# A two-layer image kernel: the last window group in a PSUM bank of its own, and a new order of TensorE's steps

## The chip, the cores and the metric

One Trainium2 chip, one of its cores. The metric is device microseconds for one execution of the whole program, the median of several runs.

## What is computed

Input is 16 images of 128 channels and 56x56 pixels. Layer 0, which the change is in, does this to each image:

```
x   = x + depthwise3x3(x)
y   = layernorm over channels(x)
q, k, v = y @ qkv_w + qkv_b
idx = for each of 49 windows (8x8 pixels) the 4 windows with the largest q_mean . k_mean
att = softmax(q_window . k_of_those_4_windows, per head, 4 heads)       # 64 x 256 per window and head
o   = att @ v_of_those_4_windows
o   = (o + depthwise5x5(v)) @ wo_w + wo_b                                # "lepe"
x   = x + o
x   = x + gelu(layernorm(x) @ mlp_w1 + mlp_b1) @ mlp_w2 + mlp_b2
```

Layer 1 begins with a 3x3 convolution, which is done in the same loop over images. The rest of it (a state-space scan over the pixels, a group norm, a residual) is a second stage of the program that starts when all 16 images are done.

## The kernel before, in words

The image stage is `layer0`. Its loop runs over 16 images (`bq`, `bg`), and every engine has its own instruction list, written out by hand, with semaphores between them. An image goes through a front (depthwise convolution on VectorE, first norm, the q, k, v products, choice of windows), the attention, a back (output projection, second norm, MLP), and the 3x3 convolution of layer 1, which TensorE does between the steps of the next image's front.

The attention takes the 49 windows in 25 **pairs** p (`PAIRS`; the last has one window). Names of its steps, used from here on:

- **gather**(p), L270: four DMAs on SP's queue (first window of the pair) and four on GpSimd's (second) copy k and v of the chosen windows from `kv` to a slot of `kvsel`. There are `SLOTS` = 3 slots. A gather waits until values(p-3) has read the slot (`s_vt`). The numbers of the windows are loaded into registers at L261 once for 3 pairs.
- **scores**(p), L782, TensorE: q times k, into four banks `bank[0]` to `bank[3]` (one for each head). It waits for the gather and until all exponentials of pair p-1 have read the banks (`s_p`).
- **maximum**(p), L517, VectorE; **exponentials**(p), L387, ScalarE; **reciprocal**(p), L524, VectorE; **share**(p), the scaling by it, two heads on VectorE (L528) and two on ScalarE (L397).
- **transposes**(p), L795, TensorE: the probabilities, into `turn` (`bank[4]`, `bank[5]`). It waits for both halves of share(p). ScalarE copies them out: **turned**(p), L406.
- **values**(p), L807, TensorE: transposes v into `bank[6]`; ScalarE copies it out: **kept**(p), L414.
- **convolve**(p), L835, and **attend**(p), L819, TensorE. Four pairs are a **group** (7 groups, the last has pair 24 alone). For a group, `bank[7]` collects five taps of the 5x5 depthwise convolution (`PTAP`; one, one, two and one tap in the group's four pairs) and the attention's products. VectorE adds the bank to `oacc`: **merge**(k), L565. The first convolve of a group, here an **opening** one, waits for the merge of the group before.
- **lepe**, L546, VectorE: the other 20 taps in three parts of the image, 25 of these 60 operations in the front and 35 spread over the pairs.

Order of TensorE in iteration p of the pair loop: scores(p), transposes(p-1), values(p-1), convolve(p-2), attend(p-2). ScalarE: exponentials(p), turned(p-1), share(p), kept(p-1). VectorE: merge of the group that ended at pair p-3 (`LAG`), reciprocal and share of p-1, maximum(p), then one or two lepe operations.

After the loop: **project**(s), L858, the output projection of strip s (8 rows of 56 pixels, 7 strips), into `bank[6]` and `bank[7]` by turns; **residual**(s), L663, VectorE; centring and squares of the second norm, L712, L362; its variance, L721; and so on. Before:

```
pe.wait_ge(s_oa, ONE + MERGES * (b + 1))
pe.wait_ge(s_lepe, ONE + LEPES * (b + 1))
project(0)
project(1)
cen(b, 0, 1)
```

so that project(0) waits for the last merge of all.

Of the kernel before, what the change touches and what calls it, by code (L numbers as in the profile page):

```python
# [15 lines left out]
NWIN, WS = 7, 8  # L16
WPIX = WS * WS
# [11 lines left out]
ONE = 1  # L29
# [22 lines left out]
def layer0(nc, d, x3_dram, ys_dram):  # L52

    ctx = ExitStack()
    with ctx:
# [91 lines left out]
        prob = sb("prob", [C, 2, HEADS, TOPK * WPIX])  # L147
        psums = sb("psums", [C, 2, HEADS])
        rinv = sb("rinv", [C, 2, HEADS])
        SLOTS = 3  # L150
        kvsel = sb("kvsel", [C, SLOTS, 2, 2, TOPK * WPIX])
        vT = sb("vT", [2 * WPIX, 2, 2, TOPK // 2, C])
        pT = sb("pT", [2 * WPIX, 2, 2 * HEADS, C])
# [99 lines left out]
        def merges(k):  # L253

            return sum(len(places(x)) for x in range(k))

        N_W = 9

# [239 lines left out]
        def _(dve):  # L498
# [60 lines left out]
            def merge(b, k):  # L559

                dve.wait_ge(s_o, ONE + b * PAIRS + ended(k) + 1)
                dve.wait_ge(s_lepe, ONE + b * LEPES + taken(ended(k) + LAG - 1))
                for r, c0, c1, at in places(k):
                    dst = oacc[:, WS * r:WS * (r + 1), WS * c0:WS * c1].rearrange("c y (w x) -> c w y x", x=WS)
                    nc.vector.tensor_tensor(  # L565
                        out=dst, in0=bank[7][:, WPIX * at:WPIX * (at + c1 - c0)].rearrange(
                            "c (w y x) -> c w y x", y=WS, x=WS), in1=dst, op=ALU.add).then_inc(s_oa, 1)

            def positions(b, n):
# [68 lines left out]
            with dve.Fori(0, NB) as bq:  # L638
                with dve.Fori(0, G) as bg:
                    b = bq * G + bg  # L640
                    for p in range(PAIRS + LAG):
                        for k in range(GROUPS):
                            if ended(k) + LAG == p:
                                merge(b, k)
                        if 1 <= p <= PAIRS:
                            share(b, p - 1)
                        if p < PAIRS:
                            largest(b, p)
                        for m in range(taken(p - 1), taken(p)):
                            lepe(b, m, p)  # L650

                    dve.wait_ge(s_x3o, ONE + 16 * b)
                    dve.wait_ge(s_cv, ONE + SN * b)

                    def second(s):
                        return x3pad[:, 1 + WS * s:1 + WS * (s + 1), 1:W + 1]

                    def strip(ap):
                        return ap.rearrange("c (y x) -> c y x", x=W)

                    def residual(s):
                        dve.wait_ge(s_wo, ONE + b * SN + s + 1)
                        nc.vector.scalar_tensor_tensor(out=second(s), in0=strip(bank[6 + s % 2][:, 0:STRIP]),  # L663
                                                       scalar=v("wo_b"), in1=x1[:, WS * s:WS * (s + 1), :],
                                                       op0=ALU.add, op1=ALU.add).then_inc(s_x2, 1)

                    residual(0)
                    residual(1)
                    residual(2)
                    for s in range(SN):  # L670
                        if s + 3 < SN:
                            residual(s + 3)
                        dve.wait_ge(s_rs, ONE + b * 2 * SN + SN + s + 1)
                        nc.vector.tensor_tensor(out=xn2[:, NWIN * s:NWIN * (s + 1), :].rearrange("c w k -> c (w k)"),
                                                in0=centred(s, True), in1=rstd[:, s % 3], op=ALU.mult
                                                ).then_inc(s_xn2, 1)
                    positions(b + 1, 0)
                    for s in range(SN):
                        positions(b + 1, s + 1)
                        dve.wait_ge(s_y2, ONE + b * SN + s + 1)  # L680
                        dve.wait_ge(s_x2, ONE + b * SN + s + 1)
                        nc.vector.scalar_tensor_tensor(out=second(s), in0=strip(bank[6 + s % 2][:, 0:STRIP]),
                                                       scalar=v("mb2"), in1=second(s), op0=ALU.add, op1=ALU.add
                                                       ).then_inc(s_x3, 1)
                    positions(b + 1, POS_TAPS - 1)
                    front(b + 1)

        @block.tensor
        def _(pe):
# [12 lines left out]
            def cen(b, s, second):  # L702
                if second:
                    pe.wait_ge(s_x2, ONE + b * SN + s + 1)
                    if s >= 3:
                        pe.wait_ge(s_xn2, ONE + b * SN + s - 2)
                    x = x3pad[:, 1 + WS * s:1 + WS * (s + 1), 1:W + 1]
                else:
                    if s >= 2:
                        pe.wait_ge(s_xn, ONE + b * SN + s - 1)  # L710
                    x = x1[:, WS * s:WS * (s + 1), :]
                nc.tensor.matmul(centred(s, second), centre[:, :], x, start=True, stop=True).then_inc(s_cen, 1)  # L712

            def var(b, s, second):
                n = b * 2 * SN + SN * second + s
                pe.wait_ge(s_sq, ONE + n + 1)
                if second and s >= 1:
                    pe.wait_ge(s_ln, ONE + n - 1)
                else:
# [48 lines left out]
            with pe.Fori(0, NB) as bq:  # L768
                with pe.Fori(0, G) as bg:
# [41 lines left out]
                    def attend(p):  # L811
                        n, u = b * PAIRS + p, p % 2
                        pe.wait_ge(s_vte, ONE + n + 1)
                        for j in range(wins(p)):
                            w = 2 * (p % GROUP) + j
                            for c in range(2):
                                for h in range(HEADS):
                                    head = slice(HD * h, HD * (h + 1))
                                    m = nc.tensor.matmul(bank[7][head, WPIX * w:WPIX * (w + 1)], vT[:, u, j, c, head],  # L819
                                                         pT[:, u, 2 * h + c, WPIX * j:WPIX * (j + 1)],  # L820
                                                         start=False, stop=(c == 1), skip_group_check=True)
                        m.then_inc(s_o, 1)
# [1 line left out]
                    def convolve(p):  # L824

                        k, step = divmod(p, GROUP)
                        steps = min(GROUP, PAIRS - GROUP * k)
                        if step == 0:
                            pe.wait_ge(s_oa, ONE + b * MERGES + merges(k))
                        for i in range(PTAP):  # L830
                            if (i + 1) * steps // (PTAP + 1) != step:
# [1 line left out]
                            dy, dx = divmod(VTAP + i, 5)  # L833
                            for x, (r, c0, c1, at) in enumerate(places(k)):
                                nc.tensor.matmul(  # L835
                                    bank[7][:, WPIX * at:WPIX * (at + c1 - c0)], wtap[:, i],
                                    vpad[:, WS * r + dy:WS * (r + 1) + dy, WS * c0 + dx:WS * c1 + dx].rearrange(
                                        "c y (w x) -> c w y x", x=WS), start=(i == 0 and x == 0), stop=False,
                                    skip_group_check=True)
# [2 lines left out]
                    pe.wait_ge(s_v, ONE + SN * (b + 1))  # L842
                    pe.wait_ge(s_ys, ONE + SN * b)
                    pe.sem_inc(s_gate, 1)
                    for p in range(PAIRS + 2):
                        if p < PAIRS:
                            scores(p)
                        if 1 <= p <= PAIRS:
                            transposes(p - 1)
                            values(p - 1)  # L850
                        if p >= 2:
                            convolve(p - 2)
                            attend(p - 2)

                    def project(s):
                        if s >= 2:
                            pe.wait_ge(s_x2, ONE + b * SN + s - 1)
                        nc.tensor.matmul(bank[6 + s % 2][:, 0:STRIP], wo[:, :], strip_of(oacc, s),  # L858
                                         start=True, stop=True).then_inc(s_wo, 1)

                    pe.wait_ge(s_oa, ONE + MERGES * (b + 1))
                    pe.wait_ge(s_lepe, ONE + LEPES * (b + 1))
                    project(0)
                    project(1)
                    cen(b, 0, 1)
                    project(2)
# [1024 lines left out]
```

## Time and profile before

| | us |
|---|---|
| median of 3 runs | 10832.1 |
| lowest, highest | 10815.46, 10833.55 |
| the profiled execution, its own time | 10800.28 |
| its span, first to last instruction | 10798.5 |

The page of the profile gives for each engine its busy time and share of the span: PE (TensorE's matmuls) 8564.2 us, 79%; DVE (VectorE) 8935.9 us, 83%; ACT (ScalarE) 6274.0 us, 58%; POOL (GpSimd) 6010.2 us, 56%. It has a strip of 40 slices of the span, 270 us each: the image stage is the first 16 of them, about one image in each. These shares are means over two stages that have nothing in common, so the image stage must be read by itself: a timeline lists instructions of one engine in order of time, with the idle time before each and what ended it, and the view of waits sums such idle times.

### The profile page before, as it was taken

The numbers are of one execution on the slowest core, as the hardware profiler recorded it, in microseconds if no ns is written. First come the engines' busy times: TensorE is split into PE (matmuls) and PEld (weight loads), VectorE is DVE, ScalarE is ACT, GpSimd is POOL, SyncE is SP. The second block draws the span as 40 slices with busy tenths as digits, with TensorE's granted clock in tenths as the row PEclk, the third lists the DMA queues.
The fourth block names the chain that finished last, engine by engine and source line by source line (L and its number), as shares of the span: only waits on it lengthen the run. The fifth ranks groups of instructions, "written<-read, shape, count | busy, mean of one in ns | idle before, by whom it ended". The sixth has DMA issues, their size and how long they took to land. (4 is left out here: it accounts for less than half of the span.)

```text
span 10798.5 us, 196681 instructions
## 1 busy us (share of the span) xinstructions
PE 8564.2 (79%) x61658; PEld 3676.9 (34%) x61658; DVE 8935.9 (83%) x10968; ACT 6274.0 (58%) x11797; POOL 6010.2 (56%) x3646
## 2 busy tenths in 40 slices
PE   6888888888888888677777777777777777778860
PEld 3555555555555555222222222222222222222210
DVE  6677777666677776799999999999999999999984
ACT  5666666666666666555555555555555555555543
POOL 2222222222222222678787877878787887887760
PEclk9999999999999999889898988898888888898875
DMA  2222222232222222111111111111111111111119
GB/s 66 67 67 67 67 67 67 72 73 68 67 67 67 67 67 67 42 33 40 33 40 33 38 34 35 38 32 40 33 39 34 36 37 32 40 32 38 35 44 267
DMA packets 855791, 591.00 MB, mean 55 GB/s; under 512 B 621424, under 2 KB 725872, under 8 KB 848464
## 3 DMA queue, kind: packets, MB, share of 16 engines
q1 hardware_dynamic: 751440, 423.61, 16.9%
q0 software_dynamic: 49152, 100.76, 2.5%
q10 hardware_dynamic: 54016, 51.91, 1.5%
q8 instruction: 615, 10.08, 0.4%
q14 instruction: 568, 4.65, 0.1%
HBM read 109.27 MB, written 103.81 MB: 20 GB/s over the span
## 5 line engine op out<-in xcount | busy, mean ns | idle before, releaser
L1161 POOL TENSOR_TENSOR b_hh<-b_hh,b_cn 128x1024 f32<-128x1024 f32 x1600 | 3834.0, 2413 | 1040.3 <-DVE b_hh L1416 1040.2
L1416 DVE TENSOR_TENSOR_SCAN b_hh<-b_dA,b_ub 128x512 f32<-128x512 f32 x3200 | 3864.9, 1208 | 0.0
L1285 ACT ACTIVATE b_dA<-b_db,b_negA 128x448 f32<-128x448 f32 x3200 | 1980.4, 634 | 1723.8 <-PE b_db L1510 1717.9
L270 POOL DMA_DIRECT2D kvsel<-kv x1536 | 1104.3, 721 | 3054.7 <-issue 2409.3
L1408 DVE TENSOR_TENSOR b_ub<-b_ub,b_bn 128x512 f32<-128x512 f32 x3200 | 2175.0, 680 | 358.2 <-PE b_ub L1510 338.2
L1510 PE MATMUL b_ub<-b_rows,b_pick 96*64 96x512 bf16 x6400 | 1398.4, 438 | 1004.3 <-DVE b_hh L1416 954.0
L1510 PEld LDWEIGHTS b_ub<-b_rows,b_pick 96*64 96x64 bf16 x6400 | 357.9, 110 | 3177.7 <-DVE b_hh L1416 2520.3
L1510 PE MATMUL b_db<-b_rows,b_pick 96*64 96x512 bf16 x6400 | 1253.5, 414 | 221.0 <-ACT b_dA L1285 217.9
L546 DVE SCALAR_TENSOR_TENSOR oacc<-vpad,vec,oacc 128x1064 f32<-128x1064 f32 (+1 forms) x934 | 1199.1, 1301 | 11.4
L1546 PE MATMUL b_acc<-b_hh,b_gather 64*32 64x512 f32 x12800 | 1047.4, 717 | 2.8 <-POOL b_hh L1161 2.8
L387 ACT ACTIVATE prob<-score,nmax 128x256 f32<-128x256 f32 (+1 forms) x1600 | 736.1, 474 | 283.5 <-DVE nmax L517 193.2
L755 PE MATMUL upper<-x3pad,wconv 128*128 128x448 f32 x2016 | 823.4, 550 | 0.0
L517 DVE TENSOR_REDUCE nmax<-score 128x2 f32<-128x512 f32 (+1 forms) x800 | 513.7, 683 | 312.8 <-PE score L782 311.3
L795 PE MATMUL turn<-ident,prob 128*128 128x128 f32 (+1 forms) x3200 | 463.5, 292 | 248.7 <-ACT prob L397 243.6
L835 PE MATMUL upper<-vpad,wtap 128*128 128x384 f32 (+6 forms) x2080 | 547.3, 396 | 15.4 <-DVE oacc L565 15.4
L755 PEld LDWEIGHTS upper<-x3pad,wconv 128*128 128x128 f32 x2016 | 387.4, 193 | 378.8 <-issue 377.9
L1510 PEld LDWEIGHTS b_db<-b_rows,b_pick 96*64 96x64 bf16 x6400 | 379.1, 113 | 393.6 <-ACT b_dA L1285 334.7
L795 PEld LDWEIGHTS turn<-ident,prob 128*128 128x128 f32 (+1 forms) x3200 | 369.5, 149 | 418.9 <-issue 418.9
L580 DVE SCALAR_TENSOR_TENSOR x<-xpad,vec,x 128x3136 f32<-128x3136 f32 x136 | 472.8, 3477 | 0.9
L594 DVE TENSOR_TENSOR xn<-score,rstd 128x448 f32<-128x448 f32 x119 | 74.0, 622 | 469.6 <-ACT rstd L373 468.5
L782 PE MATMUL score<-kvsel,qs 32*64 32x256 f32 x6272 | 288.7, 418 | 207.8 <-ACT prob L387 104.3
L397 ACT ACTIVATE prob<-prob,rinv 128x256 f32<-128x256 f32 (+1 forms) x800 | 365.9, 513 | 93.5 <-DVE rinv L524 93.4
(180 smaller groups left out, 12310.6 us busy)
## 6 DMA issues: line engine op xcount, KB each, us to landing
b_rows<-b_term SPq DMA_DIRECT2D x2400, 64.0 KB, 2.0
kvsel<-kv SPq DMA_DIRECT2D x1600, 64.0 KB, 2.0
kvsel<-kv POOLq DMA_DIRECT2D x1536, 64.0 KB, 2.0
xpad<-in_x SPq DMA_DIRECT2D x18, 1568.0 KB, 10.7
ys<-ysb ACTq DMA_DIRECT2D x16, 1600.0 KB, 8.4
b_yc<-ys SPq DMA_DIRECT2D x100, 256.0 KB, 2.7
xr<-b_xo SPq DMA_DIRECT2D x100, 256.0 KB, 2.7
x<-x3pad SPq DMA_DIRECT2D x16, 1568.0 KB, 18.1
```

The lines of the kernel that those rows point to most:

```text
L270: eng.dma_start(kvsel[:, slot, j, :, WPIX * t:WPIX * (t + 1)].unsqueeze(1), kv[:, bass.ds(at[t], 1), :, :]).then_inc((s_kv, s_kg)[j][slot] ...
L387: nc.scalar.activation(prob[rows(p), u, h], score[rows(p), h, 0:TOPK * WPIX], ACT.Exp, bias=nmax[rows(p), u, h:h + 1], accum_out=psums[row ...
L546: nc.vector.scalar_tensor_tensor(out=oacc[:, lo:up, :], in0=src, scalar=v("lepe_w", k), in1=oacc[:, lo:up, :], op0=ALU.mult, op1=ALU.add). ...
L755: m = nc.tensor.matmul(bank[6 + (s + 1) % 2][:, 0:STRIP], wconv[:, k], x3pad[:, 1 + WS * s + dy:1 + WS * (s + 1) + dy, 1 + dx:1 + dx + W], ...
L795: m = nc.tensor.transpose(turn[:, 2 * h + c, rows(p)], prob[rows(p), u, h, C * c:C * (c + 1)], ident[rows(p), rows(p)])
L835: nc.tensor.matmul(bank[7][:, WPIX * at:WPIX * (at + c1 - c0)], wtap[:, i], vpad[:, WS * r + dy:WS * (r + 1) + dy, WS * c0 + dx:WS * c1 + ...
L1161: nc.gpsimd.tensor_tensor(out=now, in0=now, in1=cn[:, par, :].unsqueeze(1).broadcast_to([C, 2, HT]), op=ALU.mult).then_inc(s_pm, 1)
L1285: nc.scalar.activation(later(dA[:, k % DEEP, :]), later(db[k % 2][:, :]), ACT.Exp, scale=negA[:, 8 * q + e:8 * q + e + 1]).then_inc(s_a, 1)
L1408: nc.vector.tensor_tensor(out=here[:, :], in0=here[:, :], in1=bn[:, (par + k // UNITS) % 3, :], op=ALU.mult).then_inc(s_bk, 1)
L1416: nc.vector.tensor_tensor_scan(hh[:, k // 2 % PDEEP, HT * (k % 2):HT * (k % 2 + 1)], dA[:, k % DEEP, :], ub[(UNITS * par + k) % 3][:, :], ...
L1510: m = nc.tensor.matmul(out[MH * h:MH * (h + 1), :], pick[:, e], rows[:, x, (par + k // UNITS) % 3, q, HT * h:HT * (h + 1)], start=True, st ...
L1546: m = nc.tensor.matmul(acc[32 * q:32 * q + 32, HT * h:HT * (h + 1)], gather[MH * h:MH * (h + 1), e], hh[MH * h:MH * (h + 1), k // 2 % PDEE ...
```

## The change

It has four parts, all of the image stage.

1. A fourth slot of `kvsel` (`SLOTS` = 4). The initial gathers are 4 pairs, not 3, and window numbers are loaded once for 4 pairs.
2. TensorE's order in an iteration: scores(p), convolve(p-2), transposes(p-1), attend(p-2), values(p-1). In an opening iteration convolve(p-2) stays behind transposes(p-1).
3. The last group (pair 24) is gathered in `bank[3]`, the bank of the fourth head's scores, when pair 24's exponentials have read it. So its convolve no longer waits for the merge of the group before. The last two merges move out of VectorE's pair loop to the places before residual(0) and before residual(1).
4. project(s) waits for just the merges that its strip's windows need (`touching`), and for what last read the bank that it writes: project(0) for kept(24), project(1) for the merge of the sixth group. project(0) stands before attend(24).

```
-        SLOTS = 3
+        SLOTS = 4
...
+        def gathering(k):
+            return bank[3] if k == GROUPS - 1 else bank[7]
+        def touching(s):
+            return merges((NWIN * (s + 1) - 1) // (2 * GROUP) + 1)
...
-                    for p in range(PAIRS + LAG):
+                    for p in range(PAIRS + 1):
                         for k in range(GROUPS):
                             if ended(k) + LAG == p:
                                 merge(b, k)
...
+                    merge(b, GROUPS - 2)
                     residual(0)
+                    merge(b, GROUPS - 1)
                     residual(1)
...
+                    if s == 2:
+                        pe.wait_ge(s_pte, ONE + PAIRS * (b + 1))
...
+                if second and s == 1:
+                    pe.wait_ge(s_oa, ONE + MERGES * (b + 1))
...
-                        if step == 0:
+                        if k == GROUPS - 1:
+                            pe.wait_ge(s_p, ONE + HEADS * (b + 1) * PAIRS)
+                        elif step == 0:
                             pe.wait_ge(s_oa, ONE + b * MERGES + merges(k))
...
-                    for p in range(PAIRS + 2):
+                    for p in range(PAIRS + 1):
                         if p < PAIRS:
                             scores(p)
+                        opens = p >= 2 and (p - 2) % GROUP == 0
+                        if p >= 2 and not opens:
+                            convolve(p - 2)
                         if 1 <= p <= PAIRS:
                             transposes(p - 1)
+                        if opens:
+                            convolve(p - 2)
+                        if p >= 2:
+                            attend(p - 2)
+                        if 1 <= p <= PAIRS:
                             values(p - 1)
-                        if p >= 2:
-                            convolve(p - 2)
-                            attend(p - 2)
                     def project(s):
-                        if s >= 2:
+                        pe.wait_ge(s_oa, ONE + b * MERGES + touching(s))
+                        if s == 0:
+                            pe.wait_ge(s_vte, ONE + PAIRS * (b + 1))
+                        elif s == 1:
+                            pe.wait_ge(s_oa, ONE + b * MERGES + merges(GROUPS - 1))
+                        else:
                             pe.wait_ge(s_x2, ONE + b * SN + s - 1)
...
-                    pe.wait_ge(s_oa, ONE + MERGES * (b + 1))
+                    convolve(PAIRS - 1)
                     pe.wait_ge(s_lepe, ONE + LEPES * (b + 1))
                     project(0)
+                    attend(PAIRS - 1)
                     project(1)
```

How the instructions stand. TensorE, an ordinary iteration (p = 24; the two taps of convolve(22) have two pieces each), before:

```order
L782 MATMUL score<-kvsel,qs 64x256 x4
L788 REGISTER_ALU
L795 MATMUL turn<-ident,prob 128x128 x8
L807 MATMUL upper<-ident,kvsel 128x128 x4
L835 MATMUL upper<-vpad,wtap 128x128
L835 MATMUL upper<-vpad,wtap 128x384
L835 MATMUL upper<-vpad,wtap 128x128
L835 MATMUL upper<-vpad,wtap 128x384
L819 MATMUL upper<-pT,vT 32x64 x16
```

and with the change:

```order
L796 MATMUL score<-kvsel,qs 64x256 x4
L851 MATMUL upper<-vpad,wtap 128x128
L851 MATMUL upper<-vpad,wtap 128x384
L851 MATMUL upper<-vpad,wtap 128x128
L851 MATMUL upper<-vpad,wtap 128x384
L802 REGISTER_ALU
L809 MATMUL turn<-ident,prob 128x128 x8
L833 MATMUL upper<-pT,vT 32x64 x16
L821 MATMUL upper<-ident,kvsel 128x128 x4
```

The taps have moved from behind both sets of transposes to the place right behind the scores, and the transposes of v (`upper<-ident,kvsel`) are now the iteration's last.

TensorE, end of the attention, from the last transposes (before) and from convolve(23) (with the change), waits and register steps left out. Before:

```order
L795 MATMUL turn<-ident,prob 128x64 x8
L807 MATMUL upper<-ident,kvsel 128x128 x2
L835 MATMUL upper<-vpad,wtap 128x128
L835 MATMUL upper<-vpad,wtap 128x384
L819 MATMUL upper<-pT,vT 32x64 x16
L835 MATMUL upper<-vpad,wtap 128x64 x5
L819 MATMUL upper<-pT,vT 32x64 x8
L858 MATMUL upper<-oacc,wo 128x448 x2
L712 MATMUL score<-x3pad,centre 128x448
L858 MATMUL upper<-oacc,wo 128x448
```

With the change:

```order
L851 MATMUL upper<-vpad,wtap 128x128
L851 MATMUL upper<-vpad,wtap 128x384
L809 MATMUL turn<-ident,prob 128x64 x8
L833 MATMUL upper<-pT,vT 32x64 x16
L821 MATMUL upper<-ident,kvsel 128x128 x2
L851 MATMUL score<-vpad,wtap 128x64 x5
L885 MATMUL upper<-oacc,wo 128x448
L833 MATMUL score<-pT,vT 32x64 x8
L885 MATMUL upper<-oacc,wo 128x448
L724 MATMUL score<-x3pad,centre 128x448
L885 MATMUL upper<-oacc,wo 128x448
```

convolve(23) now stands ahead of the last transposes; the last group's taps and products write `score` (`bank[3]`), and the first projection stands between the two.

## Rows read from the trace of the kernel before

**Rows 1.** the page: the span, and the granted TensorE clock in 40 slices (tenths)
```profile
span 10798.5 us, 196681 instructions
...
PEclk9999999999999999889898988898888888898875
```

**Rows 2.** waits, image stage, 0 to 4600 us: total us, times, longest us
```profile
PE turn L795 <- ACT prob L397: 243.6, 227, 2.2
...
PE score L782 <- DMA kvsel<-kv: 72.1, 82, 10.2
```

**Rows 3.** stretches of the second image: length, busy us (instructions) by engine, clock, DMA, GB/s
```profile
412.00:433.00 21.00, 17.27 (x300) 12.41 (x289) 18.56 (x33) 19.38 (x54) 13.55 (x19) 1.00 0.41 113
...
453.00:474.00 21.00, 17.48 (x265) 13.15 (x264) 16.62 (x31) 17.32 (x51) 11.50 (x16) 0.92 0.37 102
...
sum 124.00, PE 99.16 PEld 72.12 DVE 97.20 ACT 100.67 POOL 61.01; mean PE 16.53 PEld 12.02 DVE 16.20 ACT 16.78 POOL 10.17
```

**Rows 4.** timeline of PE, second image: start, us, instruction, [idle before <-releaser]
```profile
458.38 0.69 PE L782 MATMUL score<-kvsel,qs 32*64 32x256 f32 x16
461.26 1.09 PE L795 MATMUL turn<-ident,prob 128*128 128x128 f32 x8 [2.18 <-ACT prob L397]
...
463.00 1.91 PE L835 MATMUL upper<-vpad,wtap 128*128 128x256 f32 x4
...
465.75 0.69 PE L782 MATMUL score<-kvsel,qs 32*64 32x256 f32 x16
...
467.73 1.10 PE L835 MATMUL upper<-vpad,wtap 128*128 128x256 f32 x4
...
469.35 0.69 PE L782 MATMUL score<-kvsel,qs 32*64 32x256 f32 x16
471.37 1.06 PE L795 MATMUL turn<-ident,prob 128*128 128x128 f32 x8 [1.34 <-ACT prob L397]
...
475.69 0.69 PE L782 MATMUL score<-kvsel,qs 32*64 32x256 f32 x16 [0.42 <-DMA kvsel<-kv]
...
479.22 0.69 PE L782 MATMUL score<-kvsel,qs 32*64 32x256 f32 x16
```

**Rows 5.** timeline of DVE, second image: first and last pair's maximum
```profile
391.65 1.29 DVE L517 TENSOR_REDUCE nmax<-score 128x2 f32<-128x512 f32 x2 [3.38 <-PE score L782]
...
511.29 1.28 DVE L517 TENSOR_REDUCE nmax<-score 64x2 f32<-64x512 f32 x2
```

**Rows 6.** waits, second image's pair loop, 400 to 516 us
```profile
PE turn L795 <- ACT prob L397: 15.2, 13, 2.2
...
PE score L782 <- DMA kvsel<-kv: 2.9, 4, 1.1
```

**Rows 7.** timeline of PE: first and last wait of an opening step's transposes
```profile
403.62 1.94 PE L795 MATMUL turn<-ident,prob 128*128 128x128 f32 x8 [0.59 <-ACT prob L397]
...
502.46 1.33 PE L795 MATMUL turn<-ident,prob 128*128 128x128 f32 x8 [2.19 <-ACT prob L397]
```

**Rows 8.** timeline of ACT: first exponential of two pairs in a row
```profile
447.27 0.46 ACT L387 ACTIVATE prob<-score,nmax 128x256 f32<-128x256 f32 x1
...
451.46 0.47 ACT L387 ACTIVATE prob<-score,nmax 128x256 f32<-128x256 f32 x1
```

**Rows 9.** timeline of SP's queue around its loading of window numbers
```profile
440.82 1.36 SPq L270 DMA_DIRECT2D kvsel<-kv  x2
...
444.54 0.65 SPq L270 DMA_DIRECT2D kvsel<-kv  x1
```

**Rows 10.** line L270 (the gathers), 400 to 516 us
```profile
DMA to landing us min/median/max: 2.0/2.0/3.7
```

**Rows 11.** timeline of PE, end of the second image's attention
```profile
516.20 0.68 PE L795 MATMUL turn<-ident,prob 64*128 64x64 f32 x8
...
519.68 1.33 PE L835 MATMUL upper<-vpad,wtap 128*128 128x64 f32 x10 [0.97 <-DVE oacc L565]
...
521.79 1.77 PE L858 MATMUL upper<-oacc,wo 128*128 128x448 f32 x4 [0.42 <-DVE oacc L565]
```

More of the change, by code:

```diff
@@ L565, in merge @@
                     nc.vector.tensor_tensor(
-                        out=dst, in0=bank[7][:, WPIX * at:WPIX * (at + c1 - c0)].rearrange(
+                        out=dst, in0=gathering(k)[:, WPIX * at:WPIX * (at + c1 - c0)].rearrange(
                             "c (w y x) -> c w y x", y=WS, x=WS), in1=dst, op=ALU.add).then_inc(s_oa, 1)
@@ L818, in attend @@
                                     head = slice(HD * h, HD * (h + 1))
-                                    m = nc.tensor.matmul(bank[7][head, WPIX * w:WPIX * (w + 1)], vT[:, u, j, c, head],
+                                    m = nc.tensor.matmul(gathering(p // GROUP)[head, WPIX * w:WPIX * (w + 1)], vT[:, u, j, c, head],
                                                          pT[:, u, 2 * h + c, WPIX * j:WPIX * (j + 1)],
@@ L835, in convolve @@
                                 nc.tensor.matmul(
-                                    bank[7][:, WPIX * at:WPIX * (at + c1 - c0)], wtap[:, i],
+                                    gathering(k)[:, WPIX * at:WPIX * (at + c1 - c0)], wtap[:, i],
                                     vpad[:, WS * r + dy:WS * (r + 1) + dy, WS * c0 + dx:WS * c1 + dx].rearrange(
```

## The prediction

> **What bounds the kernel now.** The first view is the page. Its span of 10798.5 us [rows 1] holds two stages, and the change touches only the image stage, whose 16 images fill the first 16 slices, some 270 us each. I therefore left the page's shares alone and asked for stretches inside one attention [rows 3]. Of the 124 us from 391 to 515, PE is busy 99.16, DVE 97.20 and ACT 100.67: three engines at about four fifths each, none of them full. Such a loop is set by the order in which its steps wait for each other. The timeline of PE shows where [rows 4]. Between 458.38 and 479.22 lie four pairs, 20.84 us. In two of the four iterations PE stands behind the scores, 2.18 and 1.34 us, until ScalarE's share is done, while a convolve that needs nothing from ScalarE is queued behind the transposes. In the other two PE does not wait and runs scores to scores in 3.60 us (465.75 to 469.35) and 3.53 us (475.69 to 479.22). So PE's list is the path: its waits lengthen the loop, and the other engines get their idle time from it. The loop takes 119.64 us from the first to the last pair's maximum [rows 5]. All images look alike: over the stage the transposes wait 243.6 us for share, which is 15.2 an image, and the scores 72.1 us for gathers [rows 2], of which one wait of 10.2 belongs to the start; the rest is 3.9 an image. In the second image these are 15.2 and 2.9 [rows 6].
>
> **The sum, part by part, for one image.**
>
> *Order of convolve and transposes.* No matmul is added or taken away. A tap takes 1.10 us at the full clock [rows 4], and it now lies in the gap ahead of the transposes. In the second image the waits for share are 13 with 15.2 us [rows 6]. Six of them stand in opening iterations, where convolve stays behind the transposes: 0.59, 0.27, 1.42, 2.18, 2.19 and 2.19 us, together 8.84; the first and the last of them are in the rows [rows 7]. They stay, since the merge, the reciprocal and the share ahead of them keep their order. The others make 15.2 - 8.84 = 6.4 us. The longest is 1.34 us, in an iteration whose convolve has two taps, so one or two taps cover each of them: -6.4.
>
> *Fourth slot.* A gather is four issues on a queue. Two of SP's take 1.36 us, of which the last 0.6 [rows 9], so four take some 3.0, and the landing comes 2.0 us later at the median [rows 10]: 5.0 in all. With values at the end of the iteration the release comes 1.6 us later than now (tap and attend, 467.73 to 469.35 in rows 4). Three slots would then leave one iteration between release and scores, four leave two, at least 7.1 us by the short iterations above, and 9 on average. Once in three pairs now, and in four then, the numbers are loaded: the queue issues nothing from 442.18 to 444.54, 2.36 us [rows 9], a third more for four pairs, 3.1. With the 3.0 of the gather before, the queue is ready 6.1 us after one release, when the next one is already some 2 us old: 7.0 us in all against 7.1 or more. The waits for gathers go: -3.9. At the image's start one more gather is queued ahead of nothing that is needed; cost 0, since the second scores wait for exponentials there.
>
> *Clock.* In the stretch 412 to 433 the granted clock is 1.00, which is 2.4 GHz, and from 453 to 474 it is 0.92 [rows 3]: for part of it the chip grants 1.2 GHz. It comes right behind the 2.18 us wait, and the tap at 463.00 takes 1.91 us, not 1.10 [rows 4]. That iteration lasts 7.37 us. These waits are of the opening kind, so I leave them and the clock as they are: 0. Bounds: nothing, or all three of this image gone, some 1.7 us each for its transposes, tap and attend, -5.
>
> *New waits.* A faster PE meets the other engines. ACT's shortest pair is 451.46 - 447.27 = 4.19 us [rows 8]. Put together from rows 4, a late group would be 7.37 (opening, with the low clock) + 3.6 + 4.6 (two taps) + 3.6 = 19.2 us against 20.84, and ACT needs 16.8; the gain of 1.7 agrees with the waits taken out (1.34 and 0.42). In the early groups, with the full clock, the same sum is 5.7 + 3.6 + 4.6 + 3.6 = 17.5, close to 16.8, so that DVE's lepe operations and ACT will be late now and then (5.7 is 7.37 less the 1.7 of the low clock). The trace of before cannot show this wait. From below it is 0. From above it takes 6 of the 10.3 us back, if ACT and DVE give back as idle time half of what PE gains. I take +1.3, nearer to the lower end, since 119.64 - 10.3 = 109.3 us is 4.55 a pair, above ACT's 4.19.
>
> Loop: -6.4 - 3.9 + 1.3 = **-9.0 us an image** (-4.3 to -14).
>
> *End of the attention.* Before, the last transposes start at 516.20 and project(0) at 521.79 [rows 11], 5.59 us later. Between lie values, a tap, attend, a wait of 0.97 us for the merge, the last group's convolve (1.33) and attend, and again 0.42 us for a merge. With the change the tap lies ahead, both waits go, and attend(24) stands behind project(0): transposes 0.68, attend 0.6, values 0.3, convolve 1.3, in all 2.9 us. attend(24), 0.4 (521.01 to 521.37, where the wait begins), is still on the path, behind project(0). -5.59 + 2.9 + 0.4 = **-2.3**. The added waits cost nothing here: kept(24) is ready before the last convolve ends, and the sixth merge runs beside it on an idle DVE. What comes behind (norm, MLP, the next image's front) is the same work and moves forward as a whole. Bounds: -1.2, if kept(24) holds project(0); -3.5, if the waits that centring has now go too.
>
> Together 9.0 + 2.3 = 11.3 us an image, 16 images: **181 us**. The profiled execution took 10800.28 us and would take 10619; the median of the runs is 31.8 us above that execution, and 10832.1 - 181 = **10651 us** is the forecast for the median. The second stage does not change.
>
> **A rule against the trace.** The low clock follows a wait of 2.18 us and not one of 1.34 us [rows 4]. The Trainium skill says in "TensorE: Matmul & The Clock Gate", Part 1, that the gate goes to half rate after an idle stretch and back after a busy one; the trace agrees on both. Part 4 of that page says that transposes do not count as busy time in the way other matmuls do. By that, taps moved ahead of the transposes raise the activity just before them, and the low stretches could go in other iterations than I take; this is the second rival's mechanism. No row here separates transposes from other matmuls in this.
>
> **The rivals.**
>
> *ACT or DVE takes the place of the waits.* PE's transposes no longer wait for share, but its scores wait for exponentials. For it: three engines within 4 us of each other [rows 3]. Against it: ACT's 4.19 us a pair is well under the 4.98 that a pair takes now. It would leave 4.3 us of the loop's gain and 1.2 of the end's: 5.5 x 16 = 88, 10744 us.
>
> *The low clock goes too.* With PE earlier, merge and reciprocal come earlier, and the opening wait falls below what brought the clock down. That is 5 us an image more in images like this one: 16.3 x 16 = 261, 10571 us. Against it: the opening wait has the same steps in front of it.
>
> *Slower: the gathers become the bound.* values(p) is last now, and a slot is free later. If the fourth slot does not make up for that, each scores waits for its gather. The point from which it decides is a gather, issue to landing with the loading, of more than two iterations, some 8.5 us. The sum above has 7.0; landings of 3.7, the longest in rows 10, make it 8.7. If this came in every pair, as with a single iteration between release and scores, a pair would take at least 5.0 and with the loading up to 7.4, about 5.5 on average: 24 x 5.5 = 132, 12.4 us more than now, less 2.3 at the end: +10.1 x 16 = 162, 10994 us. Against it: the median landing is 2.0, and SP's queue needs 15.1 us for four pairs (12.0 and 3.1) where PE would need 17.5. The Trainium skill, "DMA: Bandwidth & Descriptors", section "Issuing engines are not separate DMA queues", says that both issuing engines share the same 16 DMA engines, which speaks against gathers further ahead; the share in use is 0.41 and 0.37 in the stretches of rows 3, so here there is room.
>
> *The change does not do what it says in the loop,* because another wait ends at the same time as each that is removed. Only the end gains: 2.3 x 16 = 37, 10795 us.
>
> **How the numbers follow.** My forecast (10600 to 10700) 0.62, low clock gone 0.15, ACT or DVE late 0.12, only the end 0.05, slower 0.04, and 0.02 for no change by a mixture of these. The range takes in the second and the first rival: 10570 to 10744. A measurement of this kernel tells about 0.2%, 22 us, from no change; all cases but the last two are faster by more. Faster 0.94, same 0.02, slower 0.04.
>
> **What would show it.** In the profile after, the waits of the transposes for share should fall from 243.6 to about 140 us over the stage, and those of scores for gathers from 72 to under 15. The first to last maximum of an image should be 110 to 111 us. Scores to scores should be about 3.6 with one tap and 4.6 with two, and still 7.4 in openings with the low clock. From the last transposes to the first projection it should be 2.9 us. I am wrong if a wait of scores for exponentials of more than 2 us an image appears, if gathers still hold the scores, or if the openings get shorter than 5.5 us.

## The result and the profile after

The changed kernel takes 10643.42 us (median of 4 runs, 10630.55 to 10650.4); the kernel before, on the same chip, takes 10823.78 us (4 runs, 10805.85 to 10833.55). The ratio is 0.9834 [0.9816, 0.9852]: 180 us faster, against 181 forecast and a forecast time of 10651. Of the experiments' runs below, one of order4_oldend's four took 12015.06 us at a granted clock of 0.68, where its other three lie between 10632.04 and 10649.96.

The page of the profile after, its span, busy times and granted clock by slice:

```profile
span 10648.6 us, 196346 instructions
...
PE 8596.3 (81%) x61658; PEld 3647.3 (34%) x61658; DVE 8923.8 (84%) x10968; ACT 6268.9 (59%) x11797; POOL 6010.0 (56%) x3646
...
PEclk9999999999999998888888888898888888888875
```

The busy times hardly differ from before: the work is the same, it is packed more tightly. The span is 149.9 us shorter than in rows 1, while the second stage begins 180 us earlier. One line of the second stage shows where the difference went. The view of one line gives, for VectorE's scan, durations in ns and the start of the first and last of the 3200; first of before, then of after:

```profile
L1416 DVE TENSOR_TENSOR_SCAN b_hh<-b_dA,b_ub x3200: 1196/1208/1215, 4401.6 to 10488.1; 128x512 f32<-128x512 f32 x189
```

```profile
L1445 DVE TENSOR_TENSOR_SCAN b_hh<-b_dA,b_ub x3200: 1194/1208/1211, 4221.5 to 10335.3; 128x512 f32<-128x512 f32 x189
```

The second stage begins at 4221.5 in place of 4401.6, 180.1 us earlier. From first to last scan it then takes 6113.8 in place of 6086.5 us in these two executions, with the same code; one of the experiments below shows how far this part can move. The waits of the image stage (0 to 4600 us) answer to rows 2:

```profile
PE turn L809 <- ACT prob L405: 136.1, 96, 2.0
...
DVE oacc L573 <- PE upper L833: 40.8, 16, 2.6
...
PE score L796 <- DMA kvsel<-kv: 15.0, 11, 10.7
```

The transposes wait 136.1 us in 96 places, one for each opening, where it was 243.6 in 227. The scores wait 15.0 us for gathers, of which 10.7 belong to the start, where it was 72.1 with 10.2 of the start. In the timeline of VectorE the first and last maximum of the second image answer to rows 5:

```profile
376.49 1.29 DVE L525 TENSOR_REDUCE nmax<-score 128x2 f32<-128x512 f32 x2 [3.35 <-PE score L796]
...
487.79 1.28 DVE L525 TENSOR_REDUCE nmax<-score 64x2 f32<-64x512 f32 x2 [0.18 <-PE score L796]
```

That is 111.30 us where it was 119.64. Averaged over the 16 images, from the records of both traces, the loop went from 118.81 to 110.76 us (-8.05), and the step from one image to the next from 262.15 to 251.11 (-11.04). The timeline of PE answers to rows 4:

```profile
438.68 0.69 PE L796 MATMUL score<-kvsel,qs 32*64 32x256 f32 x16
441.37 1.06 PE L809 MATMUL turn<-ident,prob 128*128 128x128 f32 x8 [2.00 <-ACT prob L405]
442.27 1.71 PE L851 MATMUL upper<-vpad,wtap 128*128 128x256 f32 x4
443.91 1.08 PE L833 MATMUL upper<-pT,vT 128*32 128x64 f32 x32
444.92 1.11 PE L821 MATMUL upper<-ident,kvsel 128*128 128x128 f32 x4
445.95 0.69 PE L796 MATMUL score<-kvsel,qs 32*64 32x256 f32 x16
446.57 1.20 PE L851 MATMUL upper<-vpad,wtap 128*128 128x256 f32 x4
447.61 1.03 PE L809 MATMUL turn<-ident,prob 128*128 128x128 f32 x8
448.58 0.65 PE L833 MATMUL upper<-pT,vT 128*32 128x64 f32 x32
449.16 0.66 PE L821 MATMUL upper<-ident,kvsel 128*128 128x128 f32 x4
449.75 0.69 PE L796 MATMUL score<-kvsel,qs 32*64 32x256 f32 x16
...
454.42 0.69 PE L796 MATMUL score<-kvsel,qs 32*64 32x256 f32 x16
...
458.15 0.69 PE L796 MATMUL score<-kvsel,qs 32*64 32x256 f32 x16
460.83 1.06 PE L809 MATMUL turn<-ident,prob 128*128 128x128 f32 x8 [2.00 <-ACT prob L405]
...
463.86 0.69 PE L796 MATMUL score<-kvsel,qs 32*64 32x256 f32 x16
```

From opening to opening is 19.47 us (438.68 to 458.15), where it was 20.84. Behind the opening PE waits for nothing: 3.80 and 3.73 us with one tap (445.95 to 449.75, 454.42 to 458.15), 4.67 with two. But the one-tap iterations are longer than the 3.60 and 3.53 of before. The opening takes 7.27 us with the low clock (a tap of 1.71) and 5.71 without. The same 2.00 us of wait stand ahead of both. Over the 16 images, the low level begins behind 25 of the 48 late openings (pairs 14, 18 and 22), where it was 38 of 48 in the trace of before.

### The profile page after: what moved, and what is told of

The parts are those of the page before. It is cut to its first block and busy times, and to the rows that moved or that the text cites. A ratio compares the mean times of both kernels' runs of the same rounds, so it can differ in the third digit from the quotient of the medians.

```text
span 10648.6 us, 196346 instructions
## 1 busy us (share of the span) xinstructions
PE 8596.3 (81%) x61658; PEld 3647.3 (34%) x61658; DVE 8923.8 (84%) x10968; ACT 6268.9 (59%) x11797; POOL 6010.0 (56%) x3646
## 5 line engine op out<-in xcount | busy, mean ns | idle before, releaser
L851 PE MATMUL upper<-vpad,wtap 128*128 128x384 f32 (+5 forms) x1920 | 549.3, 417 | 0.0
L809 PE MATMUL turn<-ident,prob 128*128 128x128 f32 (+1 forms) x3200 | 433.3, 281 | 136.8 <-ACT prob L405 136.1
L414 ACT ACTIVATE pT<-turn 128x1024 f32<-128x1024 f32 (+1 forms) x400 | 407.7, 1019 | 10.2 <-PE turn L809 9.1
## 6 DMA issues: line engine op xcount, KB each, us to landing
xpad<-in_x SPq DMA_DIRECT2D x18, 1568.0 KB, 10.7
```

Source lines behind the costliest of these rows:

```text
L809: m = nc.tensor.transpose(turn[:, 2 * h + c, rows(p)], prob[rows(p), u, h, C * c:C * (c + 1)], ident[rows(p), rows(p)])
L851: nc.tensor.matmul(gathering(k)[:, WPIX * at:WPIX * (at + c1 - c0)], wtap[:, i], vpad[:, WS * r + dy:WS * (r + 1) + dy, WS * c0 + dx:WS * ...
```

## Experiments

Each ratio is to the kernel before, timed on the same chip as the run it stands with. Its median was 10800.63 us beside slots4, order4_oldend, end_only and three_slots, 10824.84 beside end_shifted, values_first, even_lepe and even_values_first, and 10811.52 beside three_slots_shifted and even_mixed, so times in us of different runs compare less well than ratios. Loop and image step are means over the 16 images of a trace.

### The parts of the change, alone

**slots4** is the kernel before with `SLOTS = 4` in place of 3.

> The kernel before with a fourth slot of kvsel and nothing else. Theory P (TensorE's list is the path of the pair loop, and each wait taken off it counts in full): the waits of scores for gathers, 62 us over the stage without the one at the start, go, and the time falls by 40 to 60 us, ratio 0.9945 to 0.9965. Rival Q (the wait for the gather overlaps the wait for share that follows it, so that taking one away lengthens the other): the gather waits go and the waits of the transposes for share grow from 244 us by as much, time within 15 us of before.

Measured: 10760.96 us, ratio 0.9959 [0.9943, 0.9975]. Its waits over the image stage:

```profile
PE turn L795 <- ACT prob L397: 279.4, 247, 2.2
...
PE score L782 <- DMA kvsel<-kv: 10.7, 1, 10.7
```

All waits for gathers but the start's are gone, some 61 us, and the transposes' waits for share grew by 36 us. So more than half of what was taken from one wait came back in the next: the theory had the time right (at the lower edge of its range), and the rival had a part of the mechanism right. The loop takes 115.69 us, 3.1 less than before, though the two waits together became only 1.6 us an image shorter. The clock is a part of the rest: inside the loop the low level stands for 17.9 us an image in place of 19.5.

**order4_oldend** adds the new order of TensorE's steps to that, with the end of the attention as before:

```
-        SLOTS = 3
+        SLOTS = 4
...
+                        opens = p >= 2 and (p - 2) % GROUP == 0
+                        if p >= 2 and not opens:
+                            convolve(p - 2)
                         if 1 <= p <= PAIRS:
                             transposes(p - 1)
+                        if opens:
+                            convolve(p - 2)
+                        if p >= 2:
+                            attend(p - 2)
+                        if 1 <= p <= PAIRS:
                             values(p - 1)
```

> Fourth slot and TensorE's new order in the pair loop, but the end of the attention as before (last group in bank 7, projections behind the last merge). P: the loop of an image is as short as in the changed kernel, 110.8 us from first to last maximum, and the end from the last transposes to the first projection as before or a tap shorter, 4.6 to 5.6 us: the time is 130 to 145 us below before, ratio 0.9866 to 0.988. Rival (most of the gain is in the end): under 100 us.

Measured: 10647.43 us, 0.9858 [0.9834, 0.9881], a little below the range I gave. The loop takes 110.18 us, so the order is worth 5.5 us an image on top of the slot. The image step is 251.8 us, within 0.7 us of the whole change's: once the new order is in, parts 3 and 4 add little, and the two ratios can't be told apart. The way from the last transposes to project(0) takes 4.37 us here, 5.59 before and 2.56 with the whole change, so 1.2 of its 3.0 us come from the order too, which takes a tap out of it.

**end_only** is the whole change with three slots and the old order in the loop: parts 3 and 4 alone.

> Three slots and the old order of the loop, but the new end: last group in bank 3, project(0) ahead of attend(24), each projection waiting only for its own merges. P: the loop stays at 118.8 us an image, the end from the last transposes to the first projection falls from 5.6 us to about 3.6 (the tap is still in it), with attend(24) 0.4 us behind: 1.6 to 2 us an image, 25 to 35 us in all, ratio 0.9968 to 0.9977. Rival (the end was covered, since the norms behind it wait for something else): within 10 us of before.

Measured: 10846.94 us, 1.0043 [1.0027, 1.006], slower. Yet the image stage is shorter: the last transposes to project(0) take 3.60 us in place of 5.59, the image step is 260.2 us in place of 262.15, as expected, and the first scan starts at 4363.5 in place of 4401.6. The loss lies in the second stage, which no part of the change touches. There, waits from the first to the last scan, of before and of end_only:

```profile
ACT b_xc L1227 <- PE b_db L1465: 198.0, 99, 5.4
PEld b_db L1465 <- issue: 153.8, 395, 0.5
```

```profile
ACT b_xc L1250 <- PE b_db L1488: 286.0, 99, 6.4
PEld b_db L1488 <- issue: 236.0, 395, 3.8
```

"issue" is time in which PE waited for nothing the profile shows. The longest was 0.5 us and is 3.8. The timeline of the weight loads shows one such place:

```profile
4612.18 0.50 PEld L1488 LDWEIGHTS b_db<-b_yT,b_wtap 128*128 128x128 f32 x2 [3.37 <-issue]
```

There are 31 of them, 106.6 us together, some 185 us apart: the second stage is a loop of 32 turns, so there are as many as jumps back. The scans take 6167.8 us in place of 6086.5; in the ten traces without these stalls they take 6086.5 to 6123.5.

### Less than the change: the fourth slot taken away

**three_slots** is the changed kernel with `SLOTS = 3`.

> The changed kernel with three slots. This is the slower rival of the prediction, made to happen. P: between the release of a slot by the last step of an iteration and the scores that need it lies one iteration, 3.8 to 4.7 us, and a gather takes 5.0, with the loading of window numbers 7 to 8, so scores wait for gathers in nearly every pair, 15 to 20 us an image; the loop is 125 to 133 us, the time 10,860 to 11,000 us, slower than before (ratio 1.003 to 1.016). Rival (the slot is of no matter, since gathers run ahead anyway): within 20 us of the changed kernel, ratio 0.984 to 0.986.

Measured: 10990.55 us, 1.0182 [1.0162, 1.0202]. The ratio is above the range I gave, the time just inside it. The scores wait for gathers in 14 pairs of an image on average, not in nearly every one:

```profile
PE score L796 <- DMA kvsel<-kv: 283.9, 227, 10.2
```

Beyond the start that is 17 us an image. The loop takes 127.34 us. But this kernel has the 31 stalls too:

```profile
PEld b_db L1494 <- issue: 234.2, 395, 3.7
```

### Are the stalls a matter of where TensorE's instructions lie?

**end_shifted** and **three_slots_shifted** are those two kernels with 12 more one-column products among PE's first instructions, done once for the whole program (24 more instructions with their weight loads). They write what is already written there.

```
-            for j in range(3):
+            for j in 5 * (0, 1, 2):
```

> The kernel of end_only with twelve more one-column products ahead of TensorE's loops, which move all of TensorE's later instructions on by some dozens and cost under 5 us once. Theory F (where an instruction lies decides whether TensorE stands still at the branch back of the second stage's loop: 32 stalls of some 3.4 us in end_only and in the kernel with three slots, none before): the stalls go or move, the second stage falls from 6168 us to 6090 to 6120 between its first and last scan, and the time is 20 to 45 us below before, ratio 0.996 to 0.998. Rival (a slow second stage comes with the new end, or with the place of data on the chip): 32 stalls as in end_only, ratio 1.003 to 1.006.

> The kernel with three slots and the changed order, with TensorE's later instructions moved on by twelve one-column products, as in end_shifted. Theory F: the 32 stalls of its second stage go, that stage falls from 6167 us between its scans to 6090 to 6120, and the time from 10990 to 10900 to 10945 us; what is left over before, 75 to 115 us (ratio 1.007 to 1.011), is the waits for gathers in the image stage. Rival (the shift does nothing here, since the cause is the place of data): ratio 1.016 to 1.020.

Measured: end_shifted 10760.18 us, 0.9940 [0.9928, 0.9952]; three_slots_shifted 10895.59, 1.0085 [1.0071, 1.0099]. The same rows of both:

```profile
PEld b_db L1488 <- issue: 146.0, 395, 0.5
```

```profile
PEld b_db L1494 <- issue: 151.0, 395, 0.5
```

All 31 stalls are gone in both, and the scans take 6094.9 and 6098.1 us, 73 and 69 us less. Adding instructions made each kernel faster by 1.0% of before. Most of it is the stalls; the image stage, too, became 13 and 11 us shorter from the first maximum to the first scan, which has no explanation here. So end_only's 0.43% with the wrong sign was the code's place. With the shift, the end of the attention alone measures 0.6%. Its image step in the traces gives less, 31 us for 16 images in end_only and 45 in end_shifted. The kernel before wasn't run with the same shift, so how much of the 0.6% is the end isn't settled. The Trainium skill, "Runtime: NRT & Kernel Launch", section "Instruction fetch mechanics", says that a taken branch to a target outside the fetched pages forces a fetch before execution goes on. That fits as many stalls as jumps back. But the kernel before has as many packets on its instruction queue in the second stage as end_only has (327 and 326; end_shifted has 300, three_slots_shifted 296) and none of these stalls. So that a fetch is the cause isn't shown, only that 24 more instructions at the head of PE's list make the stalls go.

### What lengthened the iterations

**values_first** is the changed kernel with the order scores, convolve, transposes, values, attend:

```
+                            values(p - 1)
                         if opens:
                             convolve(p - 2)
                         if p >= 2:
                             attend(p - 2)
-                        if 1 <= p <= PAIRS:
-                            values(p - 1)
```

> The changed kernel with values(p-1) ahead of attend(p-2) again: scores, convolve, transposes, values, attend. Theory H (in the changed order a step behind values or transposes starts later than in the old order, 0.15 and 0.05 us, which is why an iteration of one tap takes 3.80 us and not 3.60): iterations of one tap take 3.60 to 3.65 us, the loop is 2 to 4 us shorter an image, since the wait of the openings takes a part back; time 30 to 60 us below the changed kernel, ratio to before 0.978 to 0.981. Rival (it is the convolve in its new place that costs the 0.2 us): iterations stay at 3.80 us, time within 10 us of the changed kernel.

Measured: 10605.9 us, 0.9799 [0.9786, 0.9811]. Its timeline of PE, one-tap iteration:

```profile
445.88 0.69 PE L796 MATMUL score<-kvsel,qs 32*64 32x256 f32 x16
446.50 1.20 PE L851 MATMUL upper<-vpad,wtap 128*128 128x256 f32 x4
447.54 1.03 PE L809 MATMUL turn<-ident,prob 128*128 128x128 f32 x8
448.41 0.60 PE L821 MATMUL upper<-ident,kvsel 128*128 128x128 f32 x4
448.94 0.65 PE L833 MATMUL upper<-pT,vT 128*32 128x64 f32 x32
449.52 0.69 PE L796 MATMUL score<-kvsel,qs 32*64 32x256 f32 x16
```

3.64 us in place of 3.80, from the same five steps. Compare starts with the changed kernel's: transposes to their successor 0.87 (was 0.97), values to its successor 0.53 (was 0.59), attend the same 0.58. The loop is 107.80 us, 3.0 less, and the time is inside the range of the theory. Why a step hands over later in one order than in the other, the runs don't show.

**even_lepe** leaves the order and spreads VectorE's lepe operations otherwise, so that each even pair up to 20 has two and each odd pair one; with `PACE` this changes sides at pair 13, and from there on the share that an opening waits for stands behind two of them.

```
-            return min(EARLY + int(PACE * (p + 1) + 0.999), LEPES)
+            return min(EARLY + p + 1 + min(p // 2 + 1, 11), LEPES)
```

> The changed kernel with VectorE's second lepe operation only in pairs 0, 2, 4 to 20, so that the pair before an opening iteration never has two (pairs 13, 17 and 21 had). Theory O (the opening wait of 2.0 us in the last three groups is VectorE being late by one lepe operation, and the low clock comes from that wait): the transposes of openings 14, 18 and 22 wait 0.8 us, as those of 6 and 10 do, the granted clock stays at full speed from pair 2 on, and an image takes 5 to 6.5 us less: 80 to 105 us below the changed kernel, ratio 0.974 to 0.977. Rival (ScalarE, 4.19 us a pair, takes over as the bound): waits of the scores for exponentials appear, under 50 us below the changed kernel.

Measured: 10544.09 us, 0.9734 [0.9719, 0.9748], just beyond the expected range. The waits, and an opening in the timeline of PE:

```profile
PE turn L809 <- ACT prob L405: 79.1, 96, 1.1
```

```profile
449.81 0.69 PE L796 MATMUL score<-kvsel,qs 32*64 32x256 f32 x16
451.34 1.06 PE L809 MATMUL turn<-ident,prob 128*128 128x128 f32 x8 [0.85 <-ACT prob L405]
...
454.38 0.69 PE L796 MATMUL score<-kvsel,qs 32*64 32x256 f32 x16
```

The opening takes 4.57 us in place of 5.71 or 7.27. Inside the loops the low level begins nowhere but in the first iteration, and from pair 3 on the granted clock is full in all 16 images. The stretches of 391 to 470 us, of the changed kernel and of even_lepe:

```profile
391.00:470.00 79.00, 73.20 (x1167) 51.88 (x1166) 70.16 (x125) 73.08 (x213) 50.72 (x72) 0.98 0.44 119
```

```profile
391.00:470.00 79.00, 74.56 (x1204) 53.09 (x1190) 74.75 (x131) 76.78 (x227) 51.85 (x72) 1.00 0.46 125
```

So each late opening cost 1.15 us of wait (2.00 less 0.85), and the low clock behind 25 of the 48 some 1.6 us more (7.27 less 5.71). For an image that makes 3.5 + 2.4 = 5.9 us, and the loop is 104.85 us, 5.9 less.

**even_values_first** has both edits.

> Both of the last two edits. If they add up, 120 to 150 us below the changed kernel. But ScalarE needs 4.19 us a pair, 96.4 us for 23 pairs, and with the first pair's 7.4 the loop of an image cannot be below 104 us, 6.8 us less than in the changed kernel. Theory: ScalarE becomes the bound, scores wait for exponentials by 1 to 3 us an image, and both together give only 90 to 110 us, ratio 0.973 to 0.976.

Measured: 10545.08 us, 0.9739 [0.9727, 0.9752], no better than even_lepe. The expected cause, ScalarE as the bound, isn't in the rows: the scores wait 4.4 us for exponentials in the whole stage after the first two pairs, 0.3 an image, where I had expected 1 to 3. What grew are two other waits, the transposes' and the merge's (16 times with 40.8 us in even_lepe):

```profile
PE turn L809 <- ACT prob L405: 125.9, 96, 1.5
...
DVE oacc L573 <- PE upper L833: 83.1, 95, 2.8
```

With attend last, the group ends later, so the merge waits at every group, the share behind it comes later, and the opening gives back what the short iterations gained. The next run tests this.

**even_mixed** has values ahead of attend, except in the iteration that ends a group:

```
+                        closes = p >= 2 and (p - 2) % GROUP == GROUP - 1
+                        if 1 <= p <= PAIRS and not closes:
+                            values(p - 1)
...
-                        if 1 <= p <= PAIRS:
+                        if 1 <= p <= PAIRS and closes:
                             values(p - 1)
```

> The kernel of even_lepe with values ahead of attend in all iterations but the one that ends a group (there attend stays ahead of values). In even_values_first the merge waited for attend 95 times, 83 us, against 16 times, 41 us, in even_lepe, and the opening iterations took 4.99 us, not 4.57. Theory M (attend last delays the merge, and with it the opening's transposes): the merge's waits fall back to about 16, openings take 4.5 to 4.7 us and the other iterations of one tap 3.6, an image's loop is 103.7 to 104.3 us against 104.85, where ScalarE's 4.19 us a pair stop it; 5 to 20 us below even_lepe, ratio 0.972 to 0.9735. Rival (openings are bound by something else): openings stay at 4.9 to 5.0 us and the time at that of even_lepe, within 5 us.

Measured: 10490.96 us, 0.9701 [0.9687, 0.9714], the fastest of all with a gain nearly twice that of the change.

```profile
PE turn L809 <- ACT prob L405: 81.0, 96, 1.1
...
DVE oacc L573 <- PE upper L833: 39.4, 16, 2.5
```

Merge and opening waits are back at even_lepe's, with the short iterations kept in all but the last of a group; the loop takes 102.53 us. I had expected 103.7 to 104.3, since I took ScalarE's 4.19 us a pair [rows 8] for a floor. It is none. Two first exponentials of pairs in a row, in its timeline:

```profile
438.12 0.46 ACT L395 ACTIVATE prob<-score,nmax 128x256 f32<-128x256 f32 x1
...
442.09 0.50 ACT L395 ACTIVATE prob<-score,nmax 128x256 f32<-128x256 f32 x1
```

3.97 us. ScalarE isn't faster here than before: the changed kernel's trace has 3.98 us too (428.07 to 432.05), and the trace of before has 3.99 in other images. I had read the 4.19 from one pair. ScalarE is busy 77.85 us of the 79 from 391 to 470, so here the next bound does begin: the scores wait for exponentials 5.7 us over the stage, after the first two pairs of each image.

## Why the prediction was right, point by point

**What bounds the kernel.** That PE's list is the path held: with its waits shortened, and no matmul or activation removed, the loop shortened.

**Waits for share, -6.4 an image.** Measured 5.84 to 0.06 outside the openings: -5.8. Right. order4_oldend against slots4 (-5.5 a loop) shows that it was the order that did it.

**Waits for gathers, -3.9.** Measured 61.9 to 4.3 us over the stage beyond the start, -3.6 an image. three_slots shows that the slot is needed: without it the new order waits 17 us an image for gathers.

**Clock and openings, 0.** Not quite: the opening waits went from 9.38 to 8.45 us an image, and the low level begins behind 25 openings in place of 38, that is 1.6 an image in place of 2.4, at 1.6 us each. Together that is some -2.2, inside my bounds (0 to -5). The late openings stayed, as forecast. That fewer of them were followed by the low clock I hadn't forecast, and no run shows why: in the trace of before, too, 10 of the 48 weren't, though in the second image, which I had read, all three were.

**New waits, +1.3.** This is the term that was mis-sized and of the wrong kind. No new wait came: the scores wait 0.1 us for exponentials in the whole stage after the first two pairs. Instead the iterations themselves got longer, with the same matmuls, of which I had counted nothing: I took 3.6 and 4.6 us as the length whatever the order. Without their waits and at the full clock, the 16 iterations from pair 3 to 23 that aren't openings take 2.5 us more in all, 0.09 to 0.2 each, and the six openings 0.15 us more each: +3.4. The loop: -5.8 - 3.6 - 0.9 (openings' waits) - 1.3 (clock) + 3.4 = -8.2, where the records have -8.05 and I said -9.0. That the forecast of 181 us met the measured 180 is in part luck: 2.2 us of openings and clock that I had put at 0 made up for iterations longer by 2.1 us more than the +1.3 that I had put down for something else.

One of my signs of being wrong was no sign at all, "if the openings get shorter than 5.5 us". Those of pairs 6 and 10 take 4.55 us now, but they took 4.4 and 5.1 us on average before, so they were shorter than that already.

**End of the attention, -2.3.** The timeline of PE after, answering to rows 11:

```profile
492.59 0.71 PE L809 MATMUL turn<-ident,prob 64*128 64x64 f32 x8
...
494.09 1.23 PE L851 MATMUL score<-vpad,wtap 128*128 128x64 f32 x10
495.15 0.97 PE L885 MATMUL upper<-oacc,wo 128*128 128x448 f32 x2
496.05 0.43 PE L833 MATMUL score<-pT,vT 128*32 128x64 f32 x16
```

2.56 us where it was 5.59, and I said 2.9. attend(24) follows project(0) as planned. What the image step gained beyond the loop is 11.04 - 8.05 = 3.0 us, 0.7 more than the sum. With the old end, in order4_oldend, it is 1.7 already, so the new end adds 1.3 of the 3.0.

**Rivals.** *ACT or DVE takes the place*: fell, no such wait; it shows up first in even_mixed, at 102.5 us a loop. *Low clock gone*: a part of it happened, but the late openings' waits stayed at 2.00 us, so it wasn't by the way that I described; even_lepe shows what it is worth when the opening wait falls to 0.85 us. I wrote that the opening wait has the same steps in front of it, and took that for fixed, and so missed that a table of lepe operations in VectorE's list sets it. *Slower by the gathers*: it needs three slots. Its 10994 us looks like three_slots' 10990.55, but some 70 us of that are the stalls; without them the kernel takes 84 us more than before (10895.59 against 10811.52), half of the 162 I priced. *Only the end gains*: fell for the whole change; end_shifted has the kernel with the new end alone, at -65 us (10760.18 against 10824.84), where I had put 37, with the open question of the shift as said above.

## What to carry to other kernels

Where three engines are each at four fifths, look for the wait in the in-order list of the engine whose iteration is the longest, and put there a step that depends on none of them; each buffer that is thereby held longer needs one more slot, or the gain turns into a loss. A wait that is cut may come back in part as the next one, so read all of the waits after each edit; and count an iteration's length anew in the new order, since the steps' hand-overs differ. Before a change of half a per cent is thrown away because it measures slower, look at whether the time was lost in code that it doesn't touch.

## What the runs showed of the hardware

- **The place of TensorE's code.** A loop stalled 3.1 to 3.8 us once a turn, 31 times in 32 turns (end_only, three_slots), or not at all, by 24 instructions far ahead of it (end_shifted, three_slots_shifted): 106.6 us of stalls, some 70 us of the second stage. The cause isn't shown.
- **Hand-over between small matmuls.** The same steps take 3.64 us as transposes, values, attend and 3.80 as transposes, attend, values. The step behind the transposes starts 0.87 or 0.97 us after them, depending on which it is. What makes this isn't settled.
- **The clock.** In the changed kernel a wait of 2.00 us (441.37) is followed by the low level, 1.2 GHz, and another of 2.00 us (460.83) is not, with PE busy without a break between. Of the 48 such waits, 25 are followed by the low level. After the waits of 0.83 to 0.85 us in even_lepe's openings (pairs 6 to 22) it never fell, nor after the 80 waits of 1.4 us in even_values_first.
